# A message-passing layer: table products on all 128 rows, x in eight pieces, count rows cleared by other engines

## The reference

```python
msg_in = concat([x[src], x[dst], edge], -1)            # 64 + 64 + 32
messages = relu(msg_in @ mW1 + mb1) @ mW2 + mb2        # 160 -> 128 -> 64
aggregated = segment_sum(messages, dst, 12500)
upd_in = concat([x, aggregated], -1)
out = relu(upd_in @ uW1 + ub1) @ uW2 + ub2             # 128 -> 128 -> 64
result = layernorm(x + out)                            # over the 64 features
```

## Time and profile before

| | |
|---|---|
| time, median of 3 runs | 2049.36 us (2049.04 to 2050.01) |
| time of the profiled execution | 2048.59 us |
| its span in the trace | 2046.8 us |
| busy: TensorE, VectorE, ScalarE, GpSimd | 70%, 43%, 27%, 72% |
| mean granted TensorE clock | 0.793 of full speed |
| table stage | first matmul 12.33 us, first gather 59.41 us, last store of table B landed 102.23 us |

### The profile page before, as it was taken

How to read it: one execution, slowest core, us unless ns; L and a number is a source line. 1 busy time by engine, 2 the same in 40 slices (tenths; PEclk the granted TensorE clock), 3 DMA queues, 4 the chain that set the end, 5 groups by cost and what they waited for, 6 DMA issues and landing times.

```text
span 2046.8 us, 34700 instructions
## 1 busy us (share of the span) xinstructions
PE 1438.8 (70%) x10080; PEld 1316.0 (64%) x10080; DVE 871.9 (43%) x2220; ACT 562.8 (27%) x929; POOL 1480.1 (72%) x1572
## 2 busy tenths in 40 slices
PE   7986666776666766766677767677677767667675
PEld 7976666666656666665666656566566656566664
DVE  3353333333333343333333444445444444444444
ACT  2332222222222222222222333233333333333332
POOL 0567777777777777777777777777777777777774
PEclk9997777777787687778876878787888778877877
DMA  8732323322232233223222223233223322232321
GB/s 212 206 100 79 80 78 77 82 78 78 80 80 78 78 80 80 77 78 81 79 76 72 80 78 82 75 81 79 76 78 80 80 75 81 78 80 75 82 78 46
DMA packets 167585, 173.49 MB, mean 85 GB/s; under 512 B 65654, under 2 KB 129433, under 8 KB 167209
## 3 DMA queue, kind: packets, MB, share of 16 engines
q0 software_dynamic: 50016, 102.53, 19.4%
q1 hardware_dynamic: 104088, 63.37, 11.2%
q10 hardware_dynamic: 13458, 7.31, 1.6%
HBM read 156.74 MB, written 16.31 MB: 85 GB/s over the span
## 4 chain that ended last, share of the span: by engine, by line
POOL 68%; issue 24%; PE 5%; POOLq 1%; DMA 1%; DVE 0%; ACT 0%; SPq 0%; ACTq 0%; DVEq 0%
POOL ag L223 68%; PE bank L367 4%; DMA xc<-x_t 1%; PE bank L260 0%; POOLq L209 0%; PE bank L270 0%; POOLq L220 0%; POOLq L773 0%; PE bank L634 0%; DMA ag<-src_table,slot_idx 0%; DMA dst_table<-picks 0%; DMA picks<-edge_t 0%; PE bank L247 0%; PE bank L640 0%; PE bank L274 0%
## 5 line engine op out<-in xcount | busy, mean ns | idle before, releaser
L223 POOL DMA_INDIRECT ag<-src_table,slot_idx x1563 | 1479.1, 946 | 543.8 <-issue 485.3
L270 PE MATMUL bank<-oh,hid 128*128 128x96 f32 x3128 | 533.5, 326 | 414.2 <-DVE xc L329 370.5
L270 PEld LDWEIGHTS bank<-oh,hid 128*128 128x128 f32 x3128 | 479.9, 234 | 472.7 <-ACT hid L291 425.0
L312 DVE TENSOR_TENSOR hid<-bank,ag 128x512 f32<-128x512 f32 x391 | 270.3, 691 | 886.6 <-DMA ag<-src_table,slot_idx 751.0
L260 PE MATMUL bank<-picked,picks 128*128 128x128 f32 x3128 | 582.5, 345 | 3.7 <-DMA picks<-edge_t 3.1
L291 ACT ACTIVATE hid<-hid 128x512 f32<-128x512 f32 x391 | 245.7, 628 | 1164.8 <-DVE hid L312 1164.8
L260 PEld LDWEIGHTS bank<-picked,picks 128*128 128x128 f32 x3128 | 520.7, 252 | 6.9 <-issue 3.3
L285 ACT ACTIVATE picks<-bank 96x512 f32<-96x512 f32 x391 | 226.2, 579 | 181.8 <-PE bank L247 132.3
L299 DVE TENSOR_TENSOR oh<-iota,rel 128x384 f32<-128x384 f32 x391 | 218.0, 558 | 117.9 <-PE bank L274 61.1
L247 PE MATMUL bank<-ident_bf,oh 128*96 128x128 bf16 x1564 | 193.6, 260 | 53.2 <-DVE oh L299 52.6
L247 PEld LDWEIGHTS bank<-ident_bf,oh 128*96 128x96 bf16 x1564 | 147.4, 155 | 103.4 <-DVE oh L299 65.7
(11 more groups left out here) (55 smaller groups left out, 349.4 us busy)
## 6 DMA issues: line engine op xcount, KB each, us to landing
picks<-edge_t SPq DMA_DIRECT2D x391, 64.0 KB
ag<-src_table,slot_idx POOLq DMA_INDIRECT x1563
picked<-dst_table SPq DMA_DIRECT2D x391, 48.0 KB
src_table<-ag SPq DMA_DIRECT2D x25, 256.0 KB, 3.5
dst_table<-picks SPq DMA_DIRECT2D x17, 256.0 KB, 2.6
xc<-x_t ACTq DMA_DIRECT2D x4, 800.0 KB, 16.0
resid<-x_rows SPq DMA_DIRECT2D x24, 128.0 KB
out<-resid ACTq DMA_DIRECT2D x24, 128.0 KB
```

Source lines behind the costliest of these rows:

```text
L223: pool.indirect_dma_start(out=ag[:, k, j * DH:(j + 1) * DH], out_offset=None, in_=src_table, in_offset=bass.IndirectOffsetOnAxis(ap=slot_i ...
L270: nc.tensor.matmul(ps_a[q][:, 0:WIN], hid[:, q, j * DH:(j + 1) * DH], oh[:, r, j * WIN:(j + 1) * WIN], start=(j == 0), stop=(j == TPG - 1))
L312: dve.tensor_tensor(hid[:, q, :], ps_h[q][:, :], ag[:, k, :], ALU.add).then_inc(s_pre, 1)
```

## The change

All 128 rows of `xc` and of the weight tiles enter the table products; rows 64 to 127 of both hold zeros. The weights' rows are cleared by VectorE, first thing. The count rows are cleared in eight pieces before the products, the even ones by VectorE ahead of its other work, the odd ones by GpSimd ahead of its wait for the index slots, and each product waits for its piece. They are still what the edge loop adds its counts to. x comes in eight pieces of 400 KB, which are now the first in ScalarE's queue; `w_src` is the first in SP's, and the index slots move behind the destination groups. ScalarE no longer clears count rows.

```diff
+XPARTS = 8
+XP = NODES // XPARTS
-        w_src = sb("w_src", [D, DH])
+        w_src = sb("w_src", [P, DH])
-        w_dst = sb("w_dst", [D, DH])
+        w_dst = sb("w_dst", [P, DH])
@@ pe_table
                     if w is w_src:
-                        pe.wait_ge(s_xt[at * 4 // NODES], 16)
-                        pe.wait_ge(s_xt[(at + P - 1) * 4 // NODES], 16)
-                    last = nc.tensor.matmul(banks[n % 4][:, b * DH:(b + 1) * DH], xc[0:D, at:at + P],
+                        for part in sorted({at // XP, (at + P - 1) // XP}):
+                            pe.wait_ge(s_xt[part], 16)
+                            if part % 2 == 0:
+                                pe.wait_ge(s_zero_dve, part // 2 + 1)
+                            else:
+                                pe.wait_ge(s_zero_pool, part // 2 + 1)
+                    last = nc.tensor.matmul(banks[n % 4][:, b * DH:(b + 1) * DH], xc[:, at:at + P],
                                             w[:, :], start=True, stop=True)
@@ gpsimd
+            pool.wait_ge(s_iota, 3)
+            for n in range(1, XPARTS, 2):
+                pool.memset(xc[D:P, n * XP:(n + 1) * XP], 0.0).then_inc(s_zero_pool, 1)
+            pool.wait_ge(s_zero_pool, XPARTS // 2)
             pool.wait_ge(s_first, 16)
             src_table_stored(pool)
@@ sync
+            sp.dma_start(w_src[0:D, :], mw1[0:D, :]).then_inc(s_wsrc, 16)
+            sp.dma_start(dst_g, dst_groups).then_inc(s_dstg, 16)
             sp.dma_start(slot_idx[:, :], src_first).then_inc(s_first, 16)
-            sp.dma_start(dst_g, dst_groups).then_inc(s_dstg, 16)
-            sp.dma_start(w_dst[:, :], mw1[D:2 * D, :]).then_inc(s_wdst, 16)
+            sp.dma_start(w_dst[0:D, :], mw1[D:2 * D, :]).then_inc(s_wdst, 16)
@@ scalar
-            act.dma_start(w_src[:, :], mw1[0:D, :]).then_inc(s_wsrc, 16)
-            for n in range(4):
-                part = slice(n * NODES // 4, (n + 1) * NODES // 4)
+            for n in range(XPARTS):
+                part = slice(n * XP, (n + 1) * XP)
                 act.dma_start(xc[0:D, part], x_t[:, part]).then_inc(s_xt[n], 16)
             act.dma_start(dst_i[:, :], dst_tiles).then_inc(s_dstt, 16)
             act_src_table()
             act.memzero(agg_t[:, :]).then_inc(s_zero_act, 1)
-            act.memzero(xc[D:P, NODES // 2:]).then_inc(s_zero_act, 1)
@@ vector
+            dve.memset(w_src[D:P, :], 0.0)
+            dve.memset(w_dst[D:P, :], 0.0).then_inc(s_zero_w, 1)
+            for n in range(0, XPARTS, 2):
+                dve.memset(xc[D:P, n * XP:(n + 1) * XP], 0.0).then_inc(s_zero_dve, 1)
             dve.memset(ones_bf[:, :], 1.0)
@@ vector, behind the window values
-            dve.memset(xc[D:P, 0:NODES // 2], 0.0).then_inc(s_zero_dve, 1)
@@ vector, before the edge loop
-                dve.wait_ge(s_zero_act, 2)
-                dve.wait_ge(s_zero_dve, 1)
+                dve.wait_ge(s_zero_act, 1)
+                dve.wait_ge(s_zero_dve, XPARTS // 2)
+                dve.wait_ge(s_zero_pool, XPARTS // 2)
@@ tensor
             pe.wait_ge(s_wsrc, 16)
+            pe.wait_ge(s_zero_w, 1)
             pe_table(s_a_mm, s_a_cp, w_src)
```

More of the change, by code:

```diff
@@ L150, in build @@
         s_resid = sem("s_resid")
-        s_xt = [sem(f"s_xt{n}") for n in range(4)]
+        s_xt = [sem(f"s_xt{n}") for n in range(XPARTS)]
         s_const = sem("s_const")
@@ L157, in build @@
         s_zero_dve = sem("s_zero_dve")
+        s_zero_pool = sem("s_zero_pool")
+        s_zero_w = sem("s_zero_w")
         s_zero_act = sem("s_zero_act")
```

## The result

The changed kernel takes 2034.72 us (median of 4 runs, 2033.67 to 2035.36) against 2049.69 of the kernel before (4 runs, 2049.04 to 2050.13): a ratio of 0.9927, interval 0.9910 to 0.9944. The prediction said 2030 with 2024 to 2041. One run of that repeat fell into a slower state, at 2169.39 us, and is left out of its median. The profiled execution of the changed kernel took 2035.36 us.

The account below looks back on a forecast made before the run. GpSimd's gathers were taken to bound the kernel, fixed by the first's and the 33rd's start. The 33rd moves 19.5 us, 9.4 from the earlier start and 10.1 from the closed hole, from a 2049.36 median to 2030, range 2024 to 2041.

Parts of the forecast that it names:

- The mechanism: Table matmuls: 128 rows let TensorE reach 2.4 GHz, a step taking 0.9 us, 25 steps 23 us in place of 43.
- Rival C: Table matmuls: the clock doesn't rise, only the earlier start counts, 4.8 us, giving 2044.6; chance 0.12.
- D: First 32 gathers: full DMA engines hold up their issue; at a pitch of 2.1 us the time is 2057; chance 0.03.
- B: Table B: TensorE, paced by the stores, loses its clock; 12.1 us saved, 2037; chance 0.10.
- the 80.3: Table B's stores: DMA-bound, taking 29.9 us from 48, landed by 80.3 us with 2.4 us of latency.
- The hole: GpSimd's idle 10.41 us before the 33rd gather: it closes, worth 10.1 us, that gather starting at 90.1.
- 7.4 to the gather: The handover from table B's last store landed to the 33rd gather: 7.4 us, allowing that gather at 87.7.
- the first gather: GpSimd's start after the DMA-bound source table: 50.0 us in place of 59.41, with 46 to 55 as bounds.
- Eight pieces of x: x's load: TensorE starts 4.8 us earlier, at 7.5 in place of 12.33, by itself worth nothing.
- The order on SP: SP's queue in table A: window-value wait near 15 us, stores 4 to 9 from about 20; 2 us added for starved engines.
- A: The forecast case: fast matmuls in both tables, DMA-bound stage; 2030 us, own range 2024 to 2035; chance 0.75.
- everything shifts: All behind the 33rd gather: rigid at a pitch of 1.250 us, so it moves by the same 19.5 us.

Follow-up runs that it names:

- experiment 1: The change with 64 rows again in the products of both tables, all else as changed: 2048.21 us, 0.9991 of the kernel before.
- experiment 2: The change with 64 rows in table B only, 128 in table A: 2040.64 us, 0.9947 of the kernel before.
- experiment 11: Experiment 7 with the window values' stores behind store 12, their loads and VectorE's use of them behind the tables: 2031.05 us.
- experiment 4: The change with x in four pieces behind the source weights and both queues in their old order: 2031.97 us, 0.9908 of the kernel before.
- experiment 5: The change with x still in eight pieces but both queues in their old order: 2032.53 us, 0.9912 of the kernel before.
- experiment 12: Experiment 4's kernel once more, beside the change on the same chip: 2032.62 us, 0.9913 of the kernel before.
- experiment 10: The change with the 784 KB of destination tiles loaded twice ahead of table A's copies: 2036.91 us, 0.9930 of the kernel before.
- experiment 6: The change with the 784 KB load of destination tiles moved behind table A's stores: 2034.49 us, 0.9921 of the kernel before.
- experiment 7: The change with both experiment 4's four pieces in old order and experiment 6's later destination tiles: 2032.12 us, 0.9905 of the kernel before.
- experiment 8: The kernel before, unchanged, run once more for a second profile: 2048.68 us in one run.
- experiment 9: The changed kernel repeated without alteration: 2035.07 us, 0.9923 of the kernel before.

## Why the prediction was right, and where it was off

**The mechanism held.** The table matmuls went from 418 to 275 ns with the row count and with nothing else (experiment 1), zeros in half the rows notwithstanding, and it is the clock that the rows change (experiment 2). Ten steps of table B take 9.17 us without a break, 0.92 a step where I took 0.9. Rival C had this wrong, and with it the rule of TensorE: Matmul & The Clock Gate of the Trainium skill (Part 1, What's actually happening) that sustained work lifts the clock: 43 us of it at 64 rows didn't. D was wrong too, nearly: the pitch of the first 32 gathers beside full DMA engines was 1.26 in place of 1.25 (1.31 in experiment 11). B did not happen: the granted clock did fall in table B, to 0.50 from 60 to 62 us, but was back by 64, and the table landed at 79.28, a microsecond ahead of the 80.3 that I had put down. In table A it fell more: the matmuls took 29.0 us of work and not 23; what that cost was not measured apart.

**The hole closed, as worked out.** The first index slots were refilled at 85.65, 6.4 us after the landing (I had 7.4 to the gather), long before the 93.24 at which GpSimd wanted them. Experiment 2 puts it back and shows its price, 4.4 to 5.9 us.

**The term that was mis-sized is the first gather.** I had 50.0 us, it was 52.90; with 52.90 my own sum gives 93.0 for the 33rd (93.24 measured). Of the 4.7 us between 2030 and 2034.72, 3.1 lie before the 33rd gather (93.24 against 90.1), the rest behind it. Two steps made those 2.9 us. *Eight pieces of x* said that TensorE's early start "is worth nothing by itself, the bytes are the same". It is worth less than nothing as the change makes it: the order that brings x to the front costs about 2 us at the first gather and 2.5 to 2.7 in time (experiments 4, 5 and 12). Without it the first gather comes at 50.87, near my 50.0. With it VectorE got the destination groups at 12.34 (8.47 in experiments 4 and 5), 0.4 MB less pass in 14 us, and table A's first stores are issued 5 us earlier only to land at about the same time. Why fewer bytes pass at the same share, no run shows.

*The order on SP* had ScalarE's wait at the ninth step right, but two sizes wrong. It took the first stores to land 10 to 11 us after issue; they took 19.8. And it had SP at the window values near 15 and stores 4 to 9 leaving from about 20; SP came there at 25.14 and they left from 29.88. I had blamed TensorE for SP's lateness, but in the new kernel it was SP's own issues that took the time, 8.14 us for one of them. So the backlog that was to keep the engines busy did not reach them: slots 4 to 7 lay filled and not issued, and the share fell to 0.79. How much hangs on this instant shows in a comparison of all profiles with 128 rows in table A and the old place of the window values: from the departure of stores 4 to 9 to the first gather there pass 22.96 to 23.35 us in eight profiles out of nine (29.88 to 52.90 in the change, 27.88 to 50.87 in experiment 4, 32.67 to 55.63 in 10) and 24.27 in experiment 5. Experiment 11 takes the window values out of the way and has the first gather at 47.18. That bytes ahead of the stores cost time, 0.80 MB for 2.4 to 2.9 us, experiments 6, 7 and 10 bear out; in them SP's departure moved by 2.4 to 3.0 as well, so they do not tell a bound by bytes from one by SP's issues.

Two bounds of mine do not agree: the first gather had 46 to 55 in one place and 44 to 55 in A's range. 2024 belongs to 44; 46 would give 2026. Nothing hangs on it, since 52.90 lies in both.

Rival C's price, 2044.6, was off too. The early start alone was measured: 2048.21, a gain of 1.7 and not 4.8. TensorE started 5.6 us earlier than before and ended table A 2.6 us earlier (52.69 against 55.33), having waited 1.72 us for the second piece of x and 0.56 for a slot.

**Behind the 33rd gather some of the gain is lost.** I said that everything shifts. In the profiles 16.4 us at the 33rd became 14.1 at the last gather and 13.2 in the span; by medians the kernel gained 15.0 to 15.6. The second pair of profiles (experiments 8 and 9) has 14.5 at the 33rd, 11.3 at the last and 11.2 in the span. From the 33rd to the last the kernel before took 1914.15 and 1914.55, the two profiles of the change 1916.47 and 1917.77, the ten others 1914.68 to 1918.97. The idle time between gathers is the same; the gathers themselves last longer in sum (1479.1 and 1479.5 us in the two profiles of the kernel before, 1481.7 and 1483.7 in the change's, 1480.4 in experiment 12, 1484.5 in 10). In part this is run-to-run spread: four pieces took 1915.78 and 1914.98. Whether the changed kernels' loops are really slower by 1 to 2 us, and what lengthens single gathers, stays open. In experiment 7 this took the gain: its loop needed 1917.77, 2.0 us more than experiment 4's. In experiment 6 it did not; the profiled run kept its gain to the last gather (2006.41), and of the three slower runs there is no trace.

## What to carry to other kernels

If TensorE works without a gap and its matmuls still last as long as at 1.2 GHz, look at the number of rows. At an equal clock they made no difference here (272 and 275 ns), but with 64 the clock never came back; filling them up to 128 with zeros took a step from 1.72 to 0.92 us. Then ask what stands behind the engine that was sped up: here the stores of its results, so that 33 us of matmul time saved (86.0 became 29.0 + 24.5) bought 15, of which table B's rows held 4.4 to 5.9 and table A's 2.5 when taken back one at a time, and both 13.5 when taken back together. And an engine that starts earlier on a stage bound by transfers can lose time, if the loads that let it start push others back: issue what unblocks the longest chain first, not what the first engine wants.

## What I had not expected of the hardware

- While x streamed in the changed kernel, the issue of a 256 KB store held SP's queue for 0.38 us at first and for 8.14 us three microseconds later, and all that SP issued next came as much later. What fills the queue, no run here varied.
- At a DMA share of about 1.0 the engines moved 201 to 216 GB/s while x went to 64 partitions, and 290 to 331 GB/s in windows full of stores. The share is time, not bytes; a tally of shares holds only while the mix stays the same.
- Stores of 512-byte rows issued behind nothing of their own, but beside a queue of 6,400-byte rows, took 19.8 us to land; in the old order, issued 4 to 5 us later, 13.6 beside rows of 6,400 bytes (experiment 5) and 12.0 beside rows of 12,800 (experiment 4). DMA: Bandwidth & Descriptors of the Trainium skill (Queues, rings and completion order, Arbitration) says that an engine takes its queues in turn, packet by packet, which would give the larger packets the larger share. From 13 to 30 us x's queue had 72.3% of the engines' time and the stores' 28.1%, which fits; but doubling x's rows did not slow the stores, and no run here varied the packet size of the stores.
- The granted clock has no entry before its first change. In the changed kernel it reads 1.00 beside matmuls of 421 ns until 10.7 us; from 14 to 16, where they take 421 ns again, it reads 0.56. Durations are the safer reading at the start of a trace.
